# The product of an attention kernel with its values: from three fp32r matmuls to raw fp32 operands, with the kernel rows in four buffers

## What is computed

```python
uv = jax.nn.silu(xn @ uv_w.T + uv_b)
u, v, base = (uv[..., :E], uv[..., E:2 * E], uv[..., 2 * E:])        # E = 256
base = _rope(base[:, :, None, :] * gamma[None, None] + beta)
q, k = (base[:, :, 0, :], base[:, :, 1, :])
qk = jnp.einsum('bis,bjs->bij', q, k)
kernel = jnp.square(jax.nn.relu(qk / SQRT_S + bias[None]))
out = u * jnp.einsum('bij,bje->bie', kernel, v)
return out @ o_w.T + o_b + shortcut
```

## Time and profile before

| | |
|---|---|
| median of 3 runs | 454.58 us (454.51 to 455.42) |
| the profiled execution's own time | 456.13 us |
| its span, first to last instruction | 454.3 us |
| busy over the span | PE 371.5, PEld 299.2, DVE 294.0, ACT 245.2, POOL 176.2 us |
| turns 0 to 7 of attention, as read from the timeline | from 71 to about 270 us |
| expert part | about 271 to 430 us |
| last part, transfers | about 430 to 454 us |
| mean granted TensorE clock | 0.927 of full speed; 1.00 within the loop turns of attention |

### The profile page before, as it was taken

One profiled execution on the slowest core, in us unless ns is written; L12 is line 12 of the kernel. 1 busy time (PEld: TensorE's weight loads), 2 busy tenths in 40 slices (PEclk: granted clock), 3 DMA queues, 4 the chain that ended last, 5 costly groups with the idle time before them and its releaser, 6 DMA issues.

```text
span 454.3 us, 8228 instructions
## 1 busy us (share of the span) xinstructions
PE 371.5 (82%) x2041; PEld 299.2 (66%) x2042; DVE 294.0 (65%) x726; ACT 245.2 (54%) x453; POOL 176.2 (39%) x159
## 2 busy tenths in 40 slices
PE   1168457799998989899999969999999999999800
PEld 1157435566665667566756638999999999999700
DVE  2889798988988888989899822333333333333245
ACT  0203027565676766665656715666666666666400
POOL 0486004562534526180716200444444444444500
PEclk9995567999999999999999997999999999999955
DMA  8618993000000001010100101221222212212089
GB/s 227 212 46 237 231 191 61 29 30 19 23 23 18 29 6 41 0 47 0 41 6 30 42 0 30 66 63 60 64 59 63 64 57 65 64 57 65 36 251 309
DMA packets 49792, 33.65 MB, mean 74 GB/s; under 512 B 5747, under 2 KB 46195, under 8 KB 49780
## 3 DMA queue, kind: packets, MB, share of 16 engines
q1 hardware_dynamic: 29120, 16.27, 12.8%
q10 hardware_dynamic: 16308, 8.26, 9.1%
q0 software_dynamic: 4352, 8.99, 5.5%
HBM read 17.63 MB, written 15.87 MB: 74 GB/s over the span
## 4 chain that ended last, share of the span: by engine, by line
PE 50%; DVE 21%; issue 12%; ACT 6%; ACTq 4%; DMA 4%; DVEq 2%; POOL 0%; POOLq 0%
PE bank L1133 14%; PE bank L1114 7%; PE bank L908 7%; PE bank L909 6%; PE bank L910 6%; DVE work L748 3%; PE bank L1020 3%; ACT base_qk L414 3%; DVE xs L613 3%; ACTq L356 2%; PE bank L946 2%; PE bank L1107 2%; DMA work<-results 2%; DVE qk_lo L725 2%; DVE k_lo L757 2%
## 5 line engine op out<-in xcount | busy, mean ns | idle before, releaser
L865 POOL DMA_INDIRECT slots_in<-xs,slot_now x64 | 75.2, 1176 | 124.5 <-DVE xs L634 77.9
L895 POOL DMA_INDIRECT results<-work x72 | 69.2, 960 | 109.2 <-DVE work L822 107.4
L822 DVE TENSOR_SCALAR work<-bank,work 128x128 f32<-128x128 f32 x72 | 25.2, 350 | 93.5 <-PE bank L1133 93.5
L1133 PEld LDWEIGHTS bank<-wdn,work 128*128 128x128 f32 x576 | 75.1, 191 | 6.0
L1133 PE MATMUL bank<-wdn,work 128*128 x576 | 75.7, 274 | 0.0
L499 ACT ACTIVATE work<-bank 128x512 f32<-128x512 f32 x72 | 43.1, 599 | 14.7 <-PE bank L1114 14.7
L505 ACT ACTIVATE work<-bank 128x512 f32<-128x512 f32 x72 | 43.1, 598 | 8.9 <-PE bank L910 3.4
L1114 PE MATMUL bank<-cst,work 128*128 128x128 f32 x288 | 43.9, 276 | 0.0
L908 PE MATMUL bank<-wup_lo,x_hi 128*128 x72 | 35.3, 491 | 1.0 <-DVE x_lo L813 1.0
L493 ACT CAST x_hi<-bank 128x128 fp32r<-128x128 f32 x72 | 19.0, 266 | 30.8 <-PE bank L1107 30.8
L1114 PEld LDWEIGHTS bank<-cst,work 128*128 128x128 f32 x288 | 34.2, 143 | 0.5 <-issue 0.4
(11 more groups left out here) (177 smaller groups left out, 824.1 us busy)
## 6 DMA issues: line engine op xcount, KB each, us to landing
slots_in<-spare ACTq DMA_DIRECT2D x1, 4680.0 KB, 31.7
work<-slots_in SPq DMA_DIRECT2D x36, 130.0 KB, 2.2
x_all<-in_L_attn_x SPq DMA_DIRECT2D x4, 512.0 KB, 8.7
work<-in_L_ffn_W_up SPq DMA_DIRECT2D x4, 512.0 KB, 3.5
wdn<-in_L_ffn_W_down SPq DMA_DIRECT2D x4, 512.0 KB, 7.3
work<-results SPq DMA_DIRECT2D x8, 256.0 KB, 7.2
work<-results ACTq DMA_DIRECT2D x8, 256.0 KB, 7.7
out<-x_all SPq DMA_DIRECT2D x8, 256.0 KB, 5.7
```

The lines of the kernel that those rows point to most:

```text
L865: pool.indirect_dma_start(slots_in, bass.IndirectOffsetOnAxis(slot_now[:, k, t:t + 1], 0), xs1[:, k, t, :], None).then_inc(tokens_sent, 16)
L895: pool.indirect_dma_start(results, bass.IndirectOffsetOnAxis(dest[:, at:at + 1], 0), slot_y[:, k, :], None).then_inc(returned[k], 16)
L1133: last = pe.matmul(P_Y[h][:, 0:D], hid_t[:, h, rows], wdn[:, of, c, :].rearrange("p a d -> p (a d)"), start=(c == 0), stop=(c == HC - 1))
```

## The change

`values` multiplies raw fp32 operands: one plain fp32 matmul where three fp32r matmuls were summed. So the split of `v` and of `kern` goes: L443 (four per turn on ACT), one of the two silus per half of `v` (L422 and L423 become one instruction, two fewer per turn on ACT), L757 (four per turn on DVE) and L738 (two per turn on DVE). `kern` becomes a tensor of its own with four buffers, and `kernel_square` waits for the last turn's products only at j = 0. Nothing else is moved: the order of what stays is as before. The core of the diff:

```diff
-        v_hi, v_lo = sb("v_hi", [P, TB, EU], F32R), sb("v_lo", [P, TB, EU], F32R)
+        v = sb("v", [P, TB, EU])
-        k_hi, k_lo = sb("k_hi", [P, 2, T], F32R), sb("k_lo", [P, 2, T], F32R)
+        kern = sb("kern", [P, TB, T])
...
-        kern = cut(5120, (2, T))
...
                     part = vf[:, 2 * n:2 * n + 2, :].rearrange("p t e -> p (t e)")
-                    act.activation(v_hi[:, 2 * n:2 * n + 2, :].rearrange("p t e -> p (t e)"), part, ACT.Silu)
-                    act.activation(part, part, ACT.Silu).then_inc(v_hi_made, 1)
+                    act.activation(v[:, 2 * n:2 * n + 2, :].rearrange("p t e -> p (t e)"), part, ACT.Silu).then_inc(v_made, 1)
...
-            def kernel_hi(b, j):
-                act.wait_ge(kern_made, b * TB + (j + 1))
-                act.wait_ge(av_done, START + b * TB + (j - 1) if j >= 2 else START + b * TB)
-                act.copy(k_hi[:, j % 2, :], kern[:, j % 2, :]).then_inc(k_hi_made, 1)
...
                 dve.wait_ge(ring_ready, START + b * NRING + (RING.index(f"qk{j}") + 1))
-                if j >= 2:
-                    dve.wait_ge(k_lo_made, b * TB + (j - 1))
+                if j == 0:
+                    dve.wait_ge(av_done, START + b * TB)
...
-            def kernel_lo(b, j):
-                dve.wait_ge(k_hi_made, b * TB + (j + 1))
-                dve.wait_ge(kern_made, b * TB + (j + 1))
-                dve.tensor_tensor(k_lo[:, j % 2, :], kern[:, j % 2, :], k_hi[:, j % 2, :].bitcast(F32), ALU.subtract)\
-                   .then_inc(k_lo_made, 1)
...
             def values(b, j):
-                pe.wait_ge(k_lo_made, b * TB + (j + 1))
+                pe.wait_ge(kern_made, b * TB + (j + 1))
                 if j == 0:
-                    pe.wait_ge(v_lo_made, START + b * 2 + 2)
+                    pe.wait_ge(v_made, START + b * 2 + 2)
                     pe.wait_ge(g_made, START + b * 2)
                 for e in range(2):
-                    last = product(P_AV[e][:, :], v_hi[:, j, e * P:(e + 1) * P], v_lo[:, j, e * P:(e + 1) * P],
-                                   k_hi[:, j % 2, :], k_lo[:, j % 2, :], start=(j == 0), stop=(j == TB - 1))
+                    last = pe.matmul(P_AV[e][:, :], v[:, j, e * P:(e + 1) * P], kern[:, j, :], start=(j == 0), stop=(j == TB - 1))
                 last.then_inc(av_done, 1)
```

More of the change, by code:

```diff
@@ L199, in build @@
         x2_hi_made, x2_lo_made, x1_hi_made, x1_lo_made = sem("x2_hi_made"), sem("x2_lo_made"), sem("x1_hi_made"), sem("x1_lo_made")
-        silu_b_made, ut_made, v_biased, v_hi_made, v_lo_made = (
-            sem("silu_b_made"), sem("ut_made"), sem("v_biased"), sem("v_hi_made"), sem("v_lo_made"))
+        silu_b_made, ut_made, v_biased, v_made = sem("silu_b_made"), sem("ut_made"), sem("v_biased"), sem("v_made")
         base_made, rot1_made, rot2_made, qk_made, qk_hi_made, qk_lo_made = (
             sem("base_made"), sem("rot1_made"), sem("rot2_made"), sem("qk_made"), sem("qk_hi_made"), sem("qk_lo_made"))
-        kern_biased, kern_made, k_hi_made, k_lo_made, av_done = (
-            sem("kern_biased"), sem("kern_made"), sem("k_hi_made"), sem("k_lo_made"), sem("av_done"))
+        kern_biased, kern_made, av_done = sem("kern_biased"), sem("kern_made"), sem("av_done")
         g_made = sem("g_made")
@@ L350, in _ @@
         def _(act):
-            for s in (base_made, out_t_made, sh_relu, sh_made, silu_b_made, ut_made):
+            for s in (base_made, out_t_made, sh_relu, sh_made, silu_b_made, ut_made, v_made):
                 act.sem_inc(s, START)
@@ L469, in turn @@
                 shared_square(b, 3)
-                kernel_hi(b, 2)
-                kernel_hi(b, 3)
                 if not last:
@@ L516, in _ @@
         def _(dve):
-            for s in (rx_copied, qk_made, qk_lo_made, mixed, g_made, kern_biased, x2_lo_made, x1_lo_made, v_biased, v_lo_made, rot2_made):
+            for s in (rx_copied, qk_made, qk_lo_made, mixed, g_made, kern_biased, x2_lo_made, x1_lo_made, v_biased, rot2_made):
                 dve.sem_inc(s, START)
@@ L727, in v_bias @@
             def v_bias(b):
-                dve.wait_ge(v_lo_made, START + b * 2)
+                dve.wait_ge(v_made, START + b * 2)
                 for n in range(2):
@@ L732, in v_bias @@
                                       vb_bc[:, :].unsqueeze(1).broadcast_to([P, 2, EU]), ALU.add).then_inc(v_biased, 1)
-            def v_split(b):
-                part = "p t e -> p (t e)"
-                for n in range(2):
-                    dve.wait_ge(v_hi_made, b * 2 + (n + 1))
-                    dve.tensor_tensor(v_lo[:, 2 * n:2 * n + 2, :].rearrange(part), vf[:, 2 * n:2 * n + 2, :].rearrange(part),
-                                      v_hi[:, 2 * n:2 * n + 2, :].rearrange(part).bitcast(F32), ALU.subtract)\
-                       .then_inc(v_lo_made, 1)
             def kernel_square(b, j):
                 dve.wait_ge(ring_ready, START + b * NRING + (RING.index(f"qk{j}") + 1))
-                if j >= 2:
-                    dve.wait_ge(k_lo_made, b * TB + (j - 1))
+                if j == 0:
+                    dve.wait_ge(av_done, START + b * TB)
                 at = (TB - 1 - j) * P
-                dve.scalar_tensor_tensor(kern[:, j % 2, :], ring(f"qk{j}")[:, :], float(S) ** -0.5,
+                dve.scalar_tensor_tensor(kern[:, j, :], ring(f"qk{j}")[:, :], float(S) ** -0.5,
                                          bias_t[:, at:at + T], ALU.mult, ALU.add).then_inc(kern_biased, 1)
                 dve.wait_ge(kern_biased, START + b * TB + (j + 1))
-                dve.scalar_tensor_tensor(kern[:, j % 2, :], kern[:, j % 2, :], 0.0, kern[:, j % 2, :],
+                dve.scalar_tensor_tensor(kern[:, j, :], kern[:, j, :], 0.0, kern[:, j, :],
                                          ALU.max, ALU.mult).then_inc(kern_made, 1)
-            def kernel_lo(b, j):
-                dve.wait_ge(k_hi_made, b * TB + (j + 1))
-                dve.wait_ge(kern_made, b * TB + (j + 1))
-                dve.tensor_tensor(k_lo[:, j % 2, :], kern[:, j % 2, :], k_hi[:, j % 2, :].bitcast(F32), ALU.subtract)\
-                   .then_inc(k_lo_made, 1)
             def gate(b):
@@ L793, in turn @@
                     mix(b - 1)
-                kernel_lo(b, 2)
-                kernel_lo(b, 3)
                 if not last:
```

5 lines of the change are left out of this document (removed).

## The result

| | median us | fastest and slowest | ratio to before, 95% interval |
|---|---|---|---|
| changed kernel, timed first | 459.98 | 458.6 to 464.47 | 1.0141 (1.0082 to 1.0200) |
| the same kernel, on a second chip | 449.12 | 447.28 to 449.28 | 0.9855 (0.9820 to 0.9889) |
| the same kernel, on a third chip, put there twice | 451.42 and 450.70 | 449.72 to 453.10 | 0.9918 (0.9882 to 0.9953) and 0.9903 (0.9872 to 0.9933) |

The kernel before took 454.58, 455.28 and 455.39 us on these three. When it was first timed the changed kernel was slower, where the forecast had faster. The later measurements of the same kernel, unedited, had the other sign. So there are two questions: what held the first one back, and where the rest of the forecast stands.

A forecast was written before the change was run, and what follows sets the result against it. No engine was always busy; a path through PE's first half, then ACT and DVE, bound the turn. Turn 0 -2.8, turns 1 to 6 -5.4, turn 7 +0.4 took 454.58 to 446.8 us; range 445 to 449, chance 0.58.

The forecast's parts named there:

- the second half of the turn: From ACT's L414 through DVE's L711 to L725: L414 0.9 earlier, DVE's chain unchanged, so next scores 0.9 earlier.
- rival for slower: Two cases: new matmuls of two 592 ns records, 466 us (chance 0.08); shared reads on DVE's chain, 457 us (0.04).
- POOL's adding of rows: Shared reads: POOL's L872 falls on DVE's L638 or L725, 1.5 a turn, 457 us; chance 0.04.
- The wait at 186.72: Transposes behind values(b, 0) stop waiting for DVE's L748 and start 0.91 earlier; base_part 0.85 earlier.
- The products: Each values block on PE, two products, goes from 1.43 to 1.71 us: +0.28, four times a turn.
- four blocks of turn 7: Last turn's values: 16 records of 0.43, 6.86 us in place of 6.44, so +0.4.
- The four thirds from the Trainium skill: Fp32 takes four passes against three: blocks cost 1.90 for 1.43, the turn's first half ending 0.4 us later; forecast rejected it.
- Turn 0: Third scores 0.9 earlier without two silus, transposes from 88.05 to 85.3, base_part from 90.08 to 87.4: -2.8 us.
- The sum: Turn 0 -2.8, turns 1 to 6 -5.4, turn 7 +0.4: -7.8 us, giving 446.8; nothing elsewhere.
- The slack of PE ahead of the scores: PE ready at 199.1, chain arriving at 199.9: 0.8 us, hiding the +0.56 of values(b, 2) and (b, 3).
- the busiest engine by the Trainium skill's measure: Optimise DVE first: six instructions, 3.6 us a turn, go; rival then has PE as bound, 442.6 us, chance 0.17.

The follow-up runs named there:

- i2: f3 with the later sends of f2, on the third chip: 453.07 us, ratio 0.9946.
- h4: f2 unedited, run again on the third chip: 447.85 us, ratio 0.9845.
- h1: The changed kernel, unedited, first of two copies on the third chip: 451.42 us.
- i3: f3 with three fp32r matmuls per product of values in place of one plain fp32 matmul, low parts left out, third chip: 447.08 us, ratio 0.9822.
- f4: The kernel before with plain fp32 matmuls in values, all work of the split kept but its results unused: 456.75 us, ratio 1.0036.
- f3: The changed kernel with PE pausing ahead of shared_down(b, 2) until DVE has turned the next batch's base rows: 462.86 us, ratio 1.0183.
- h2: f3 unedited, run again on the third chip: 455.43 us, ratio 0.9979.
- first and third sets: First: four edits of the changed kernel, without it beside them, 445.14 to 455.80 us. Third: the changed kernel on the second chip and two edits, 449.00 to 449.73.
- second, fourth and fifth sets: Second: f1 to f4, 447.50 to 462.86 us. Fourth: two copies of the changed kernel, f3 and f2, unedited, third chip. Fifth: f3, i2, i3 there.
- f1: The changed kernel with POOL's sends held until the first base activation L411, starting 1.3 us later than on the second chip: 448.57 us, ratio 0.9863.
- f2: The changed kernel with POOL's sends held until the third base activation L411, starting 2.7 us later than on the second chip: 447.50 us, ratio 0.9819.

## Why the prediction was wrong

**The step that failed** is the second half of the turn: "What follows on DVE ... is unchanged ... So the next scores start 0.9 earlier if PE is there", with PE "there at 199.1; the chain arrives at 199.9". It took for granted that every reader of a PE product can start when the product ends. In the first measurement ACT stood idle for up to 2.16 us ahead of L430 with its product done, PE's first or second scores waited for L430 behind them (8.6 us in ten waits), and the clock halved behind two of these gaps. Turns that were to take 23.8 took 25.1 to 28.2. Neither rival for slower is it: the new matmuls step by 0.43, not 1.05 and more a product, and POOL's adding of rows does not sit on the chain.

**What the runs show of its cause.** Two things came together wherever the increments were late: one of the chips that has them, and a row of sends in which neither of the first two is stretched. On such a chip the later sends of i2, and of h4 against h1, ended them, and so did i3. Whether the plain fp32 products are a party is not shown: i3 took them away, but its second send is stretched too, and no run has fp32r products beside unstretched sends on such a chip. f4 has plain fp32 products with stretched sends, on f3's chip, and no late increment. The pause ahead of `shared_down` makes them stronger: the waits of L430 for L878 sum to 11.3 us in h2, against 4.0 in h1, by a way that is not shown; of the 6.1 us between the turns of these two some 3.8 is the pause itself. The change moved the sends against DVE's work: before, the second send was stretched in every turn. Two of them, before and then after (first execution):

```profile
191.40 1.15 POOL L865 DMA_INDIRECT slots_in<-xs,slot_now  x1 [11.99 <-DVE xs L634]
192.86 1.88 POOL L865 DMA_INDIRECT slots_in<-xs,slot_now  x1 [0.30 <-issue]
```
```profile
196.01 0.98 POOL L833 DMA_INDIRECT slots_in<-xs,slot_now  x1 [13.46 <-DVE xs L621]
197.29 0.96 POOL L833 DMA_INDIRECT slots_in<-xs,slot_now  x1 [0.30 <-issue]
```

**What stays open.** How the sends hold back an increment, and what differs between chips, no run shows. Nor is it shown that the recording by the profiler has no part, since every execution was recorded, and the traces give reason to ask. Between 78 and 240 us every semaphore update of PE, ACT and DVE has its record within 0.06 us of its instruction's end in the traces of the first and third sets (468 to 498 in each) and of the kernel before (537). In the first execution 95 of 451 have none, and in the traces of the second, fourth and fifth sets 50 to 103 of 460 to 535, nearly all of them while the sends run (91 of the 95). So the chips with late increments are the chips whose traces lack such records; yet f1, f2, f4, h4, i2 and i3 lack them too, without being late. The first set's chip is like the second chip in this, which is one more reason that its runs tell nothing. The Trainium skill ("TensorE: Matmul & The Clock Gate", The cost: per-tile semaphore tail) has increments of PE serialize at about 26 ns each. What is seen here, 2 to 3 us, is some hundred times that, so this rule does not explain it.

**The rest, where no increment was late** (second chip, profiled execution against that of before). *The wait at 186.72*: the transposes start 9.84 behind the first scores, forecast 9.72, since the four transposes ahead of `values(b, 0)` take 0.43, as L994 above, and not 0.35; `base_part` 11.84, forecast 11.84. *The products*: 0.43 a record, as forecast, and 6.87 for the four blocks of turn 7 (forecast 6.86, before 6.44), seen here:

```profile
250.54 7.03 PE L981 MATMUL bank<-kern,v 128*128 128x512 f32 x16
257.41 1.88 PE L967 MATMUL bank<-work,shdn 128*128 128x512 f32 x4
```

The four thirds from the Trainium skill that the prediction weighed against this row would have made it 7.6 or so (1.90 a block); the row taken was right. One record has a mean of 593 ns, and they step by 430, the answer to the earlier trace rows:

```profile
L981 PE MATMUL bank<-kern,v 128*128 128x512 f32 x128 | 58.6, 593 | 0.0
```

*Turn 0*: its third scores start 1.50 behind the first (forecast 1.5), its transposes 7.68 behind (forecast 7.8, before 10.55), the answer to the earlier trace rows; the first start at 78.08:

```profile
79.58 0.40 PE L876 MATMUL bank<-qk_lo,qk_hi 128*128 128x512 f32 x1
...
85.76 0.60 PE L944 MATMUL bank<-cst,xs 128*128 128x128 f32 x4
```

*The sum*: turn 0 -2.92 (forecast -2.8), turns 1 to 6 together -5.27 (forecast -5.4), from the last turn's scores to the end +0.75 (forecast +0.4), and +0.58 ahead of attention, where nothing was forecast: -6.9 of spans, for -7.8. The time follows it: 0.9855 of 454.58 is 448.0, for 446.8. *The slack of PE ahead of the scores* was mis-sized, 0.4 in place of 0.8, because the first projection record of 256 columns behind `shared_down` takes 0.52 to its next, not half a step, as it did in the kernel before (195.91 to 196.43); it cost nothing. That DVE, the busiest engine by the Trainium skill's measure in the prediction, lost 4.9 us of work and the turn 0.9 is as the forecast had it: DVE bounds only where the chain runs through it.

**The best version** is f2: 447.50 and 447.85 us on two chips, 0.9819 (0.9788 to 0.9851) and 0.9845 (0.9805 to 0.9884) of before, the first on the chip of f3's 462.86, where the changed kernel itself was not timed. On the third chip all its executions (447.08 to 449.69) lie below all of the changed kernel's (449.72 to 453.10). It holds its time on both chips on which f3 showed late increments (462.86 and 455.43 us there).

## What to carry to other kernels

When a change removes waits, look at what else now starts together: here it let a row of indirect sends run unstretched, and where that met the wrong chip it cost more than the change had brought. Starting the sends 2.7 us later, on an engine with slack, made the gain safe. Each set of experiments needs the kernel under study beside it: two sets without it led me to a cause in the program that a single control refuted. And an edit that takes one suspect away can move another: compare the rows of all suspects in both traces before calling it a test of one.

## What the runs showed of the hardware

- A reader of a PE product can start 3.3 us after the matmul's end, with ACT idle for 2.15 of them, while PE's scores start within 0.06 of the end of the L430 that they wait for. The same program on three chips shows 16.9, 4.0 and 0 us of such waits in attention.
- POOL's second send and DVE's L698 started within 0.04 us of each other in two turns of f3: in one the send took 2.01 us and L698 1.22, in the other 0.96 and 1.29. Only the second turn ended late.
- Traces of the same program kept different shares of its semaphore updates: in attention all on the second chip, and all but 95 of 451 and 98 of 489 on the first and the third (h1).
- Two gaps of PE on either side of the first scores (0.46 and 1.09, 0.82 and 1.12) were followed by 3.3 us at half the clock; a pair of 0.88 and 1.08 in turn 1, and the single gap of 1.15 in turn 4, were not.
- On the path of a turn, eight 128x512 products in plain fp32 cost 0.38 us more than in three fp32r matmuls each (23.80 and 23.42), while the turn with the work of the split kept took 0.8 to 1.0 us more than without it (24.62 to 24.76 in f4 from turn 2 on, against 23.80).
